# Evicting each 128-row output tile whole by one engine instead of in two halves by two engines

## What is computed

```
# h: token embedding of the last 16 tokens, one hidden layer, logits
emb = wte[shifted indices]                 # 16 shifts, 64 channels each
h   = tanh(x_emb @ w1 + b1) @ w2 + b2      # 64 hidden -> 1024
# autocorrelation attention on the normalised rows, residual
h   = h + attn(layernorm(h))
# linear layer with low-rank updates on the normalised rows, residual
n   = layernorm(h)
h   = h + n @ W.T + bias + sum_e coeffs_e * scales_e * (n @ A_e.T) @ Bf_e.T
out = h                                    # (16, 1024, 1024), float32
```

## Time and profile before

| | |
|---|---|
| median of three runs | 428.76 us (427.09 to 428.93) |
| span of the profiled execution | 440.3 us |
| PE busy in it | 409.3 us, 93% |
| DVE busy | 282.6 us, 64% |
| ACT busy | 239.9 us, 54% |
| POOL busy | 229.5 us, 52% |
| evictions on ACT, L500 | 128, mean 779 ns |
| evictions on DVE, L676 | 128, mean 807 ns |

### The profile page before, as it was taken

How to read it: one execution, slowest core, us unless ns; L and a number is a source line. 1 busy time by engine, 2 the same in 40 slices (tenths; PEclk the granted TensorE clock), 3 DMA queues, 4 the chain that set the end, 5 groups by cost and what they waited for, 6 DMA issues and landing times.

```text
span 440.3 us, 6477 instructions
## 1 busy us (share of the span) xinstructions
PE 409.3 (93%) x1886; PEld 318.6 (72%) x1886; DVE 282.6 (64%) x606; ACT 239.9 (54%) x359; POOL 229.5 (52%) x287
## 2 busy tenths in 40 slices
PE   2589969999999999999999999999999999999793
PEld 2465347888878777787878787878778878888582
DVE  3614866668585857677766758485857666775742
ACT  2215035666565656565656666565657556664632
POOL 6752383837566573737473847556465827131300
PEclk9999999999999999999999999999999999999998
DMA  5586002545545546354553544644636445454565
GB/s 99 186 266 255 1 16 67 218 143 222 185 192 208 199 154 247 116 223 176 189 210 125 228 165 194 211 191 172 233 110 263 145 190 209 163 218 175 207 253 228
DMA packets 27685, 79.86 MB, mean 181 GB/s; under 512 B 6187, under 2 KB 7483, under 8 KB 27669
## 3 DMA queue, kind: packets, MB, share of 16 engines
q1 hardware_dynamic: 23572, 75.46, 44.7%
q0 software_dynamic: 4096, 4.20, 4.9%
HBM read 12.40 MB, written 67.12 MB: 181 GB/s over the span
## 4 chain that ended last, share of the span: by engine, by line
PE 63%; POOL 13%; DVE 12%; issue 7%; ACT 2%; POOLq 1%; DMA 1%; another core or an unknown queue 1%; SPq 0%; DVEq 0%; ACTq 0%
PE o_ps L1064 35%; PE conv_ps L989 10%; PE conv_ps L992 5%; POOL beta L448 4%; POOL inv_std L438 4%; PE mix_ps L1096 2%; DVE u_rows L783 2%; DVE obuf L676 2%; PE sum_ps L1147 2%; PE sum_ps L1084 2%; DVE et_hl L754 2%; PE et_ps L1074 1%; DVE prod L773 1%; POOL var_eps L446 1%; POOL var_eps L436 1%
## 5 line engine op out<-in xcount | busy, mean ns | idle before, releaser
L500 ACT ACTIVATE obuf<-o_ps,mean_sb,a_sb 128x512 f32<-128x512 f32 x128 | 99.7, 779 | 98.4 <-PE o_ps L1064 83.4
L403 POOL DMA_INDIRECT gathered<-in_wte,idx_now x128 | 128.7, 1006 | 44.1 <-issue 34.9
L676 DVE TENSOR_SCALAR obuf<-o_ps,a_sb,mean_sb 128x512 f32<-128x512 f32 x128 | 102.6, 807 | 53.1 <-PE o_ps L1064 37.9
L1064 PE MATMUL o_ps<-w_hi,u_hi 128*128 128x512 f32 x256 | 104.8, 409 | 3.4 <-DVE obuf L676 2.5
L1064 PE MATMUL o_ps<-w_lo,u_hi 128*128 128x512 f32 x256 | 101.2, 395 | 0.0
L1064 PE MATMUL o_ps<-w_hi,u_lo 128*128 128x512 f32 x256 | 101.1, 395 | 0.0
L1064 PE MATMUL o_ps<-extra,xT 128*128 128x512 f32 x256 | 101.0, 394 | 0.0
L989 PE MATMUL conv_ps<-et_hl,shift_hi 128*128 128x512 f32 (+1 forms) x264 | 70.3, 409 | 5.1 <-DVE hT L764 2.8
L436 POOL TENSOR_SCALAR var_eps<-var 128x8 f32<-128x8 f32 x16 | 8.0, 501 | 110.1 <-DVE var L808 102.8
L989 PEld LDWEIGHTS conv_ps<-et_hl,shift_hi 128*128 128x128 f32 x264 | 50.2, 198 | 16.0 <-DVE hT L764 3.0
L1064 PEld LDWEIGHTS o_ps<-w_hi,u_hi 128*128 128x128 f32 x256 | 48.2, 188 | 17.8 <-issue 6.2
(11 more groups left out here) (133 smaller groups left out, 443.9 us busy)
## 6 DMA issues: line engine op xcount, KB each, us to landing
out<-obuf SPq DMA_DIRECT2D x63, 1024.0 KB, 4.0
h_all<-in_wT SPq DMA_DIRECT2D x4, 1024.0 KB, 9.9
gathered<-in_wte,idx_now POOLq DMA_INDIRECT x128
aT_sb<-in_aT SPq DMA_DIRECT2D x1, 1024.0 KB
bfT_sb<-in_bfT SPq DMA_DIRECT2D x1, 1024.0 KB, 13.6
obuf<-in_w SPq DMA_DIRECT2D x2, 256.0 KB
extra<-xbar_twice SPq DMA_DIRECT2D x1, 512.0 KB
out<-obuf SPq DMA_DIRECT2D x1, 512.0 KB
```

What stands on the lines that cost most here:

```text
L403: pool.indirect_dma_start(gathered[p][:, i, :], None, wte, bass.IndirectOffsetOnAxis(ap=idx_now[p][:, i:i + 1].bitcast(U32), axis=0),).the ...
L500: nc.scalar.activation(obuf[:, q, i % 2, 0:512], o_ps[:, 2 * (i % 2), :], ACT.Identity, bias=mean_sb[pc][:, i:i + 1], scale=a_sb[pc][:, i: ...
L676: nc.vector.tensor_scalar(obuf[:, q, i % 2, 512:L], o_ps[:, 2 * (i % 2) + 1, :], a_sb[pc][:, i:i + 1], mean_sb[pc][:, i:i + 1], ALU.mult, ...
L1064: last = mm(o_ps[:, 2 * (i % 2) + n, :], lhsT, rhs[:, 512 * n:512 * (n + 1)], start=(f == 0), stop=(f == len(factors) - 1))
```

## The change

Even tiles are evicted whole by ACT and odd tiles whole by DVE, each with one instruction of 1024 columns over both banks of the slot. The counters are now one for even and one for odd tiles; product i waits for the one of its own slot. In ACT's order tile_out(0), (2), (4), (6) become even_out(0) to (3) at the places of tiles 0, 2, 4 and 6, and tiles 1, 3, 5, 7 leave it; in DVE's order the odd ones stay at their places and the even ones leave. SP waits for the two counters as before, and stores the very last tile in one transfer of 512 KB. Everything else is unchanged. The diff, cut where it only takes out a call:

```diff
@@ SP @@
-                        sp.wait_ge(oa_kept, NT * c + 2 * q + 2)
-                        sp.wait_ge(ov_kept, NT * c + 2 * q + 2)
+                        sp.wait_ge(even_kept, NT // 2 * c + q + 1)
+                        sp.wait_ge(odd_tile_kept, NT // 2 * c + q + 1)
                         sp.dma_start(out_pairs[bass.ds(4 * c + q, 1)].rearrange("a p i o -> (a p) i o"),
                                      obuf[:, q, :, :]).then_inc(stored[q], 16)
                     if last:
-                        sp.wait_ge(oa_kept, NT * c + 7)
-                        sp.wait_ge(ov_kept, NT * c + 7)
+                        sp.wait_ge(even_kept, NT // 2 * c + 4)
                         sp.dma_start(out_tiles[NT * c + 6], obuf[:, 3, 0, :]).then_inc(stored[3], 16)
-                        sp.wait_ge(oa_kept, NT * c + 8)
-                        sp.dma_start(out_tiles[NT * c + 7][:, 0:512], obuf[:, 3, 1, 0:512]).then_inc(stored[3], 16)
-                        sp.wait_ge(ov_kept, NT * c + 8)
-                        sp.dma_start(out_tiles[NT * c + 7][:, 512:L], obuf[:, 3, 1, 512:L]).then_inc(stored[3], 16)
+                        sp.wait_ge(odd_tile_kept, NT // 2 * c + 4)
+                        sp.dma_start(out_tiles[NT * c + 7], obuf[:, 3, 1, :]).then_inc(stored[3], 16)
@@ ACT @@
-            def tile_out(c, pc, i):
-                q = i // 2
-                if i % 2 == 0:
-                    ge(act, stored[q], 16 * c)
+            def even_out(c, pc, q):
+                i = 2 * q
+                ge(act, stored[q], 16 * c)
                 act.wait_ge(o_done, NT * c + i + 1)
-                nc.scalar.activation(obuf[:, q, i % 2, 0:512], o_ps[:, 2 * (i % 2), :], ACT.Identity,
-                                     bias=mean_sb[pc][:, i:i + 1], scale=a_sb[pc][:, i:i + 1]).then_inc(oa_kept, 1)
+                nc.scalar.activation(obuf[:, q, 0, :], o_ps[:, 0:2, :].rearrange("p a n -> p (a n)"), ACT.Identity,
+                                     bias=mean_sb[pc][:, i:i + 1], scale=a_sb[pc][:, i:i + 1]).then_inc(even_kept, 1)
...
                 if back:
-                    tile_out(c, u, 2)
-                    tile_out(c, u, 3)
+                    even_out(c, u, 1)
...
                 if back:
-                    tile_out(c, u, 4)
+                    even_out(c, u, 2)
                 if front:
                     take_tanh(0)
-                if back:
-                    tile_out(c, u, 5)
                 if back and not front:
-                    tile_out(c, u, 6)
+                    even_out(c, u, 3)
...
                 if back and front:
-                    tile_out(c, u, 6)
-                if back:
-                    tile_out(c, u, 7)
+                    even_out(c, u, 3)
@@ DVE @@
-            def tile_out(c, pc, i):
-                q = i // 2
-                if i % 2 == 0:
-                    ge(dve, stored[q], 16 * c)
+            def odd_out(c, pc, q):
+                i = 2 * q + 1
+                ge(dve, stored[q], 16 * c)
                 dve.wait_ge(o_done, NT * c + i + 1)
-                nc.vector.tensor_scalar(obuf[:, q, i % 2, 512:L], o_ps[:, 2 * (i % 2) + 1, :], a_sb[pc][:, i:i + 1],
-                                        mean_sb[pc][:, i:i + 1], ALU.mult, ALU.add).then_inc(ov_kept, 1)
+                nc.vector.tensor_scalar(obuf[:, q, 1, :], o_ps[:, 2:4, :].rearrange("p a n -> p (a n)"), a_sb[pc][:, i:i + 1],
+                                        mean_sb[pc][:, i:i + 1], ALU.mult, ALU.add).then_inc(odd_tile_kept, 1)
...
-                if back:
-                    tile_out(c, u, 4)
                 if mid and not in_step(1, g, u):
                     scale_h()
                 if not front and not mid:
                     give_verdict()
                 if back:
-                    tile_out(c, u, 5)
-                if back and not front:
-                    tile_out(c, u, 6)
+                    odd_out(c, u, 2)
@@ PE @@
-                    ge(pe, oa_kept, NT * c + i - 1)
-                    ge(pe, ov_kept, NT * c + i - 1)
+                    ge(pe, odd_tile_kept if i % 2 else even_kept, NT // 2 * c + i // 2)
```

More of the change, by code:

```diff
@@ L266, in tower_kernel @@
         o_done = sem("o_done")
-        oa_kept = sem("oa_kept")
-        ov_kept = sem("ov_kept")
+        even_kept = sem("even_kept")
+        odd_tile_kept = sem("odd_tile_kept")
         stored = [sem(f"stored{q}") for q in range(4)]
@@ L362, in step @@
                     if last:
-                        sp.wait_ge(oa_kept, NT * c + 7)
-                        sp.wait_ge(ov_kept, NT * c + 7)
+                        sp.wait_ge(even_kept, NT // 2 * c + 4)
                         sp.dma_start(out_tiles[NT * c + 6], obuf[:, 3, 0, :]).then_inc(stored[3], 16)
-                        sp.wait_ge(oa_kept, NT * c + 8)
-                        sp.dma_start(out_tiles[NT * c + 7][:, 0:512], obuf[:, 3, 1, 0:512]).then_inc(stored[3], 16)
-                        sp.wait_ge(ov_kept, NT * c + 8)
-                        sp.dma_start(out_tiles[NT * c + 7][:, 512:L], obuf[:, 3, 1, 512:L]).then_inc(stored[3], 16)
+                        sp.wait_ge(odd_tile_kept, NT // 2 * c + 4)
+                        sp.dma_start(out_tiles[NT * c + 7], obuf[:, 3, 1, :]).then_inc(stored[3], 16)
             steps(sp, step, lambda: None, lambda: None)
             for q in range(4):
-                sp.wait_ge(stored[q], 16 * (NSEQ + 2 * (q == 3)))
+                sp.wait_ge(stored[q], 16 * (NSEQ + (q == 3)))
             sp.wait_ge(flag_set, 1)
@@ L531, in step @@
                 if back:
-                    tile_out(c, u, 0)
+                    even_out(c, u, 0)
                 if mid:
@@ L539, in step @@
                     keep_et_hi()
-                if back:
-                    tile_out(c, u, 1)
                 if front:
@@ L801, in step @@
                 if back:
-                    tile_out(c, u, 1)
+                    odd_out(c, u, 0)
                 if mid and in_step(1, g, u):
@@ L813, in step @@
                 if back:
-                    tile_out(c, u, 2)
-                if back:
-                    tile_out(c, u, 3)
+                    odd_out(c, u, 1)
                 if mid:
@@ L858, in step @@
                     add_shifts(1)
-                if back and front:
-                    tile_out(c, u, 6)
                 if back:
-                    tile_out(c, u, 7)
+                    odd_out(c, u, 3)
             def after_step0():
```

## The result

The changed kernel takes 441.21 us (median of 4 runs, 437.94 to 442.98), the kernel before 427.92 us (426.44 to 428.93) beside it: a ratio of 1.028, 95% interval 1.022 to 1.034. The change costs 13.3 us where the forecast had 5.7, and the time is above the upper end of the range, 438.0. The direction was right, the size was not.

A forecast was written before the change was run, and what follows sets the result against it. PE was taken to set the pace, nearly or wholly, with DVE and ACT mattering only where PE waits for their queues. 14 x 0.46 = 6.4, less 1.2, plus 0.45 gave +5.7 us: 434.4 us, range 429.5 to 438.

The forecast's parts named there:

- (1): Durations of a whole-tile eviction: 1.35 us on DVE and 1.20 us on ACT.
- The rival of longer evictions: Evictions across two banks cost more, 1.35 us on ACT and 1.45 on DVE: 439.4 us; chance 0.12 shared with POOL's rival.
- (2): Tile 0 whole on ACT: copy of h and DVE's moments work 0.42 us later, hidden in the middle kind of step.
- (3): Tile 1 whole on DVE: PE loses 0.46 us at product 3 (middle steps 0.54); scaled rows 0.2 at most, priced zero.
- POOL's chain is late too: Rival: the 0.2 us at the scaled rows is paid every step, 437.2 us; chance 0.12 shared with longer evictions.
- (4): Tiles 2 and 4 on ACT, 3 and 5 on DVE: nothing on the path, 0 us.
- (5): Tile 6 whole on ACT just fits before the next product 0: 0 us, anything above 1.24 us paid in full.
- (6): Last but one step: wait of 1.5 us at product 6 goes, tile 5 and split of u late next; -1.2 us.
- (7): End of the program: last tile by DVE alone, 0.54 us later, stored in one transfer; +0.45 us.
- (8): SyncE and semaphores: pair transfers wait for two counters as before, buffer fills come much later; 0 us.
- rivals with no wait: Product 3 never waits for tile 1, so only the last but one step and the end count: 428.6 us; chance 0.14.
- the fixed cost on the path: Rival: one DVE instruction for two saves 0.26 us a pair on the path each step: 425.1 us; chance 0.06.

The follow-up runs named there:

- AVHHHHHH: The kernel before with only tile 0 evicted whole by ACT and tile 1 whole by DVE, tiles 2 to 7 in halves: 439.89 us, ratio 1.025.
- HHAVAVAV: The changed kernel with tiles 0 and 1 evicted in halves by both engines as before, tiles 2 to 7 whole: 429.08 us, ratio 1.000.
- VAVAHHHH: The kernel before with tiles 0 and 2 whole by DVE, 1 and 3 whole by ACT, 4 to 7 in halves: 440.04 us, ratio 1.026.

## Why the prediction was wrong

(1) *Durations: right.* 1.35 and 1.20 us forecast, 1.344 and 1.208 measured, 64 each. The rival of longer evictions is out.

The Trainium skill, on the page ScalarE: Activation LUTs (what ACT_TABLE_LOAD costs), gives an ACTIVATE 186 ns + 0.833 ns per column and about 93 ns for each per-row operand. With two of them that is an estimate of 1.225 us for 1024 columns, near the 1.208 measured.

(2) *Tile 0 delays the copy of h: right in size, wrong in place.* The moments work on DVE started 2.03 us into the step instead of 1.60. I held this hidden in the middle kind of step, behind 1.6 us that the plain runs don't have; there it counts in every step.

(3) *Product 3: right.* Forecast 0.46 a step; measured 0.51 in the step shown, and 23.36 - 22.96 = 0.40 in an outer step of AVHHHHHH, which has only this wait. It formed in 13 of the 14 steps; the first loses 0.05 there. With tile 0 or tile 1 alone PE is 0.15 us late at most, so it needed both delays, as the slack of 0.50 says.

*The second wait, in the same step (3): this is where the prediction failed.* I worked out 0.2 us a step for the scaled rows and priced it at zero, on the ground that the late step had shown PE unheld. Measured are 0.33 us at L1123 and 0.20 more until the convolution starts (0.80 us behind the transposes' start instead of 0.60), 0.53 in all, in each of the ten inner steps, and about 0.3 in all in each of the four outer ones. That is 6.5 us where the sum had nothing, and where the rival "POOL's chain is late too" had 2.8.

The reason for the zero was wrong: the late step was the wrong witness. It lies behind POOL's loop. The kernel before, run again, has the same chain inside and outside it (timeline of POOL, the first two lines inside):

```profile
210.76 0.23 POOL L446 TENSOR_SCALAR var_eps<-var 128x8 f32<-128x8 f32 x1 [0.20 <-POOL var L444]
211.17 1.93 POOL L448 TENSOR_TENSOR beta<-var_eps,minus_half 128x8 f32<-128x8 f32 x1 [0.18 <-POOL var_eps L446]
...
348.08 0.23 POOL L446 TENSOR_SCALAR var_eps<-var 128x8 f32<-128x8 f32 x1
348.39 1.67 POOL L448 TENSOR_TENSOR beta<-var_eps,minus_half 128x8 f32<-128x8 f32 x1
```

Inside, beta ends 6.51 us or more behind the variance instead of 5.63 to 5.66. About 0.6 us of that are gaps: POOL stands 0.18 to 0.20 us between dependent instructions where it stands 0.08 to 0.1 outside. The rest, 0.26 or more, is the last power, 1.93 us instead of 1.67, which inside meets DVE's splits of h. Ten of the 14 steps are of that kind; the nearly 1 us is the slack that I took for granted. Whether the loop causes the gaps stays open: inside it the kernel also puts a semaphore increment behind each of these waits, which the other steps don't have.

And my own trace had better witnesses. The middle steps of the profile ahead of the prediction are inside the loop, and they hold the second wait in full (timeline of PE, the step of the earlier trace rows):

```profile
225.22 0.39 PE L1064 MATMUL o_ps<-extra,xT 128*128 128x512 f32 x1
...
225.79 0.66 PE L1147 MATMUL sum_ps<-ident_sb,u_rows 128*128 128x128 f32 x4 [0.19 <-DVE u_rows L783]
```

PE was free at 225.22 + 0.23 = 225.45 and started 0.34 us late.

The wait is that large because of what a late beta sets off: the scaling is released together with POOL's copy and takes 1.08 us instead of 0.68. My own had it: the chain holds L783 for the same 1.09 us. I read that as the instruction's length, not as a collision. So the 0.2 us already held the collision. It lacked 0.13 us at the transposes and the 0.20 us of the row factors, which stand behind the scaling in DVE's queue. Moving the copy away gave back 5.2 us in the steps.

In the kernel before the collision is avoided only because DVE is still busy with its half of tile 4 when beta comes. Inside the loop the lateness of beta alone undoes that: AVHHHHHH keeps tile 4 in halves, and its scaling takes 1.08 us in all ten inner steps. In its outer steps beta comes in time, the scaling takes 0.68 us, and PE doesn't wait for the rows. In the changed kernel it takes 1.08 us in the outer steps as well, and they cost 0.33 us more (23.69 against 23.36): tile 4 has left DVE's queue, which I wrote of as a relief, and beta is later too (6.54 us behind the variance against 6.05), beside the splits.

(4) *Tiles 2 to 5 at zero: nearly right.* HHAVAVAV is at 1.000, with 0.13 us more in inner steps. Its scaling meets the copy as well (1.08 us) but ends before PE comes; the row factors behind it are late (0.71 to 0.74 us to the convolution instead of 0.60).

(5) *Tile 6 just fits: right.* In the changed kernel ACT's tile 6 runs from 231.28 to 232.49; with the 0.45 it frees the slot at 232.94, and the second matmul of product 0 ran at 232.97, in line with its neighbours.

(6) *The last but one step: right.* The wait at product 6 is gone. From that step's transposes of h to product 0 of the last step the changed kernel takes 16.48 us against 17.76, so -1.28 where -1.2 was forecast. What is late next is as named, the split of u, and tile 5 on DVE:

```profile
415.43 0.50 PE L1040 MATMUL o_ps<-w_hi,u_hi 128*128 128x512 f32 x1 [0.18 <-DVE obuf L663]
...
418.35 0.47 PE L1040 MATMUL o_ps<-w_hi,u_hi 128*128 128x512 f32 x1 [0.79 <-DVE u_lo L832]
```

(7) *The end: right.* From there to the end 22.76 us against 22.17, so +0.6 where +0.45 was forecast. The last eviction is longer (1.34 us, from 433.64), and one issue takes the place of two:

```profile
435.01 0.34 SPq L367 DMA_DIRECT2D out<-obuf  x1
```

(8) *SyncE: right.* PE's list of waits names no store.

*The sum again, with what was measured:* the product 3 wait, 13 x 0.46 = 6.0; the second wait, 10 x 0.53 = 5.3 in inner steps and 4 x 0.3 = 1.2 in outer ones; together 12.5 against 12.6 seen in the steps. Less 1.28, plus 0.6: 11.8 of the 13.3. The rest lies ahead of these steps or between executions, and stays open. The rival "POOL's chain is late too" had the right wait, at less than half its size. The rivals with no wait and with the fixed cost on the path are out: DVE is busy 10.4 us less than in the kernel before run again (268.6 against 279.0), and the full steps are longer all the same.

## What to carry to other kernels

An engine with idle time is not free at every place of its queue: price a longer eviction by what stands behind it, to the end of that queue, before its own busy time is counted. A slack has to be read in the kind of step that repeats most, here the one inside POOL's loop, and a delay that is "0.2 at most" belongs into the sum when the step repeats 14 times. When an instruction that was kept waiting by its own queue becomes ready on a semaphore, look at who else that semaphore releases.

## What the runs showed of the hardware

DVE's multiplication of 128x512 with both operands in SBUF takes 0.68 us alone and 1.08 us when POOL's copy of 128x512 (0.60 us) starts 0.07 us before it; when the copy has just ended, it takes 0.68. A row factor of 128x8 goes from 0.17 to 0.55 us beside the same copy. It holds the other way too: POOL's squares of 128x8 take 0.20 us and, while DVE splits h (two operands in SBUF), 0.37 to 0.74 us. Evictions out of PSUM on DVE kept their 1.34 us throughout the changed kernel.

The Trainium skill has this on the page SBUF — State Buffer, in the section Who interferes with whom: a DVE instruction with two SBUF inputs contends with a GpSimd instruction that reads SBUF, and whichever comes second blocks until the first is done. The trace agrees in kind. In size the second waits somewhat less than a full block would make it: 0.60 - 0.07 + 0.68 gives 1.21 us, against 1.08 measured.

POOL's chain of seven small instructions, from the variance to beta, lasted 6.25 us inside its loop and 5.63 outside where it met none of DVE's splits (VAVAHHHH), and up to 6.90 inside and 6.54 outside where it did. What made the moments product of the first profile reach DVE about 1 us late was in none of the later runs, and stays open.
